# A third buffer for the decay factors of a selective scan, in SBUF beside two in PSUM

## The reference, cut to what matters

```python
A_bar = jnp.exp(delta[..., None] * A)                 # decay factors
Bx = delta[..., None] * Bm[:, :, None, :] * xb[..., None]
def step(h, inp):
    a_t, bx_t, c_t = inp
    h = a_t * h + bx_t
    y_t = jnp.sum(h * c_t[:, None, :], axis=-1)
    return (h, y_t)
...
y = y + xb * Dp
out = y * jax.nn.silu(z) @ W_out
```

## Time and profile before

| | |
|---|---|
| time, median of 3 runs | 2658.17 us (2652.7 to 2659.58) |
| the profiled execution | 2653.91 us, its span 2651.9 us |
| VectorE busy | 2265.5 us (85%) |
| TensorE busy | 2309.5 us (87%) |
| GpSimd busy | 1728.4 us (65%) |
| ScalarE busy | 1669.0 us (63%) |
| granted TensorE clock, mean | 0.95 of full speed |

### The profile page before, as it was taken

How to read it: one execution, slowest core, us unless ns; L and a number is a source line. 1 busy time by engine, 2 the same in 40 slices (tenths; PEclk the granted TensorE clock), 3 DMA queues, 4 the chain that set the end, 5 groups by cost and what they waited for, 6 DMA issues and landing times. The chain is left out here.

```text
span 2651.9 us, 34212 instructions
## 1 busy us (share of the span) xinstructions
PE 2309.5 (87%) x11520; PEld 1586.2 (60%) x11520; DVE 2265.5 (85%) x2232; ACT 1669.0 (63%) x3332; POOL 1728.4 (65%) x2042
## 2 busy tenths in 40 slices
PE   7778889888898988888988888888888875999997
PEld 5566667676666666757666666666666322444443
DVE  2399999999999999899999999999999835888886
ACT  2567676667667676767676767676766534555554
POOL 0278787878787878778787778787878711222221
PEclk8889999999999999999999999999998987999999
DMA  4102020202010110102020202020104621111110
GB/s 186 72 1 72 9 76 6 76 5 80 16 65 21 61 53 28 65 17 73 9 72 10 72 10 72 10 76 5 72 10 189 233 83 56 60 64 66 59 52 24
DMA packets 48299, 151.74 MB, mean 57 GB/s; under 512 B 8069, under 2 KB 8965, under 8 KB 45198
## 3 DMA queue, kind: packets, MB, share of 16 engines
q1 hardware_dynamic: 48142, 149.76, 15.9%
HBM read 132.37 MB, written 17.37 MB: 56 GB/s over the span
## 5 line engine op out<-in xcount | busy, mean ns | idle before, releaser
L472 POOL TENSOR_TENSOR ring<-ring,Cbc 128x512 f32<-128x512 f32 x1024 | 1283.1, 1275 | 44.5 <-POOL carry L465 0.4
L864 DVE TENSOR_TENSOR_SCAN ring<-a_ps,ring 128x1024 f32<-128x1024 f32 x512 | 1168.0, 2281 | 106.7 <-ACT a_ps L702 105.2
L702 ACT ACTIVATE a_ps<-delta,nA 128x255 f32<-128x255 f32 x2048 | 852.9, 468 | 380.3 <-DVE ring L864 379.4
L1069 PE MATMUL yT_ps<-ident,ring 128*128 128x128 f32 x4096 | 588.1, 284 | 163.5 <-POOL ring L472 160.0
L1069 PEld LDWEIGHTS yT_ps<-ident,ring 128*128 128x128 f32 x4096 | 475.0, 145 | 282.2 <-POOL ring L472 241.9
L856 DVE TENSOR_TENSOR ring<-u_ps,Bbc 128x1024 f32<-128x1024 f32 x512 | 619.7, 1210 | 16.0 <-PE yT_ps L1069 9.3
L1035 PE MATMUL work<-xb,big 128*128 128x256 f32 x2048 | 476.8, 385 | 10.1 <-ACT zs L560 10.1
L1035 PEld LDWEIGHTS work<-xb,big 128*128 128x128 f32 x2048 | 385.5, 193 | 79.5 <-issue 16.9
L465 POOL TENSOR_TENSOR carry<-ring,half 128x4 f32<-128x4 f32 x512 | 127.1, 248 | 361.2 <-DVE ring L864 359.7
L1051 PE MATMUL work<-Wout,xb 128*128 128x512 f32 x512 | 237.7, 599 | 0.0
L1414 POOL TENSOR_TENSOR m<-m,pows 128x1 f32<-128x1 f32 x64 | 34.2, 549 | 311.4 <-DVE m L1546 311.4
(11 more groups left out here) (197 smaller groups left out, 2508.1 us busy)
## 6 DMA issues: line engine op xcount, KB each, us to landing
Bbc<-bc_rows SPq DMA_DIRECT2D x64, 512.0 KB, 4.6
Cbc<-bc_rows SPq DMA_DIRECT2D x64, 512.0 KB, 3.7
xT<-in_xT SPq DMA_DIRECT2D x16, 514.0 KB, 3.5
x_rows<-x2row SPq DMA_DIRECT2D x32, 256.0 KB, 2.0
xp<-x_rows SPq DMA_DIRECT2D x32, 256.0 KB, 2.7
xx<-in_x SPq DMA_DIRECT2D x32, 256.0 KB, 3.0
out_rows<-orow SPq DMA_DIRECT2D x32, 256.0 KB, 2.0
delta<-in_c_w SPq DMA_DIRECT2D x6, 1024.0 KB, 5.3
```

What stands on the lines that cost most here:

```text
L472: nc.gpsimd.tensor_tensor(hp, hp, Cbc[:, G * g + GP * c:G * g + GP * c + GP, :], ALU.mult)\
L702: r = nc.scalar.activation(a_ps[q % 2][:, i, 1:T], delta[:, par, dt, 1:T], ACT.Exp, scale=nA[:, dt, s:s + 1])
L864: dve.tensor_tensor_scan(ring[:, q % RING, :, :].rearrange("p g t -> p (g t)"), a_ps[q % 2][:, :, :].rearrange("p g t -> p (g t)"), ring[: ...
L1069: r = pe.matmul(yT_ps[:, tt, :], ring[:, q % RING, i, P * tt:P * tt + P], ident[:, :], is_transpose=True, start=False, stop=(g == NG - 1 a ...
```

## The change

A third decay buffer `a_sb` is laid into columns 6144 to 7167 of `big[0]`, in SBUF. The slots take the three buffers in turn by the running slot number, so every third slot uses the one in SBUF. ScalarE's wait goes from the scan of slot q - 2 to that of q - 3. `y0k`, which lay in these columns, moves to columns 5632 to 6143. The f_w1 piece for columns 6144 to 7167 is now sent after the last scan. The first column of the new buffer is cleared once.

```diff
-        y0k = big[0][:, 6 * DI:6 * DI + 2 * T].rearrange("p (b t) -> p b t", b=2)
+        y0k = big[0][:, 5 * DI + D:6 * DI].rearrange("p (b t) -> p b t", b=2)
+        a_sb = big[0][:, 6 * DI:7 * DI].rearrange("p (g t) -> p g t", g=G)
...
+        a_of = [a_ps[0], a_ps[1], a_sb]
+        NA = len(a_of)
...
-                        if 2 <= c < 9:
+                        if 2 <= c < 8:
...
+                    sp.wait_ge(s_scan, NQ * NBLK)
+                    sp.dma_start(big[0][:, 6 * DI:7 * DI], f_w1[:, 6 * DI:7 * DI]).then_inc(s_big[0], 16)
...
-                        act.wait_ge(s_aclr, 3)
-                    wait(act, s_scan, NQ * k + q - 1)
+                        act.wait_ge(s_aclr, 4)
+                    wait(act, s_scan, NQ * k + q - NA + 1)
...
-                        r = nc.scalar.activation(a_ps[q % 2][:, i, 1:T], delta[:, par, dt, 1:T], ACT.Exp,
+                        r = nc.scalar.activation(a_of[(NQ * k + q) % NA][:, i, 1:T], delta[:, par, dt, 1:T], ACT.Exp,
...
-                                           a_ps[q % 2][:, :, :].rearrange("p g t -> p (g t)"),
+                                           a_of[(NQ * k + q) % NA][:, :, :].rearrange("p g t -> p (g t)"),
...
+                        dve.memset(a_sb[:, :, 0:1], 0.0).then_inc(s_aclr, 1)
```

## The result

The changed kernel takes 2809.7 us in the median (2808.7 to 2812.06, 4 runs) against 2656.8 of the kernel before, run beside it (2652.7 to 2659.58, 4 runs): 1.0578 times as long, 95% interval 1.056 to 1.0596, or 153 us more. The forecast was 2785, with 2655 to 2880 as its range. The forecast rise of 127 us came out as 153.

The account below looks back on a forecast made before the run. VectorE was followed as the bounding engine, with GpSimd becoming full too. VectorE's 94 us and GpSimd's 67 us gave a middle of 127, other parts 0: 2653.9 + 127 = 2781 profiled, 2785 median, range 2655 to 2880.

Parts of the forecast that it names:

- The run-ahead gives nothing: ScalarE's longer run-ahead: 0 to 10 of VectorE's 93.7 us waits for factors come back, taken as 0.
- The scan is held as L835 is: Scans with two SBUF operands and GpSimd's multiplies block each other, like u product L835; GpSimd loses 2.05 us a scan.
- VectorE's own wait: VectorE's 170 scans with two SBUF operands each wait 0.55 us for GpSimd's running multiply: 94 us.
- GpSimd's term: GpSimd loses 349 us against 340.0 of reserve, 58 of it unusable: 9 + 58 = 67 us rise by GpSimd alone.
- The sum: Whole kernel: 127 us, the middle between 94 (stalls fall together) and 161 (they add), on 2653.9 profiled.
- ScalarE's writes into SBUF: ScalarE's activations for every third slot take 468 ns into SBUF as into PSUM: 0.
- y0k, the memset, the moved f_w1 piece: Moved copy, one start-up memset and a weight piece sent after the last scan, landing before it is wanted: 0.
- the scan that isn't held: Rival at VectorE's SBUF scans: they stay at 2.28 us, total 2648 to 2658, or 2564 at best; chance 0.14.
- Held but covered: Rival: scans are held but the waits fall into idle time, +9 us or less, 2658 to 2667; chance 0.05.
- GpSimd keeps its turn: Rival: a scan waits to the end of GpSimd's multiply pair, 1.73 us each, 294 us, 2952; chance 0.07.
- The fourth: Rival: GpSimd's delay reaches TensorE, then ScalarE, stretching each block's 3.6 us stall; 32 us on top, 2817; no chance given.

Follow-up runs that it names:

- e2_psum_constant: Changed kernel, but every third slot's scan reads a constant column in PSUM instead of the third buffer; run-ahead kept: 2653.2 us, 0.9981 of the kernel before.
- e1_no_runahead: Changed kernel with ScalarE's wait put back to the scan of slot q - 2; every third slot still reads factors from SBUF: 2820.8 us.
- e4_silu_later: Kernel before, with ScalarE's SiLU moved from slot 17 to slot 18, behind the factors of slot 17: 2654.3 us, 0.9987.
- e8_every_fifth: Changed kernel with only every fifth slot's factors in SBUF (102 scans), without the longer run-ahead: 2738.8 us, 1.0299 of the kernel before.
- e3_every_second: Changed kernel with every second slot's factors in SBUF (256 scans), without the longer run-ahead: 2871.0 us, 1.0793 of the kernel before.
- e11_after_xdp: Changed kernel with the product of xb and Dp moved from GpSimd to ScalarE: 2786.3 us, 1.0491 of the kernel before.
- e7_short_after: Changed kernel with GpSimd multiplying only 128 of 256 positions: 2671.3 us; the kernel before with the same short multiply: 2608.2 us.
- e5_swapped: Against the kernel before: both factor buffers in SBUF, products of u and B in PSUM, ring of three slots: 2673.8 us, 1.0051.
- e12_after_memset: Changed kernel with GpSimd's multiply replaced by a memset that writes SBUF and reads nothing: 2576 us, one run.

## Why the prediction was right

- **The run-ahead gives nothing, since the late factors hang on TensorE.** Right. With the collision away it gives 5 us, inside the 0 to 10 (e2_psum_constant), with the collision 6 to 11 (e1_no_runahead), and the waits for factors are 93.7, 93.6 and 92.4 us with two buffers, three, and three with the collision. The step from the earlier trace rows, to ask what ended ScalarE's own idle time in front of the late factors, is what told this in advance. e4_silu_later adds that ScalarE's order can move these waits, but not the time.
- **The scan is held as L835 is.** Right, in form and in the size of one stop: 1.98 us for a pair, forecast 2.05; VectorE's scans from 2.28 to 3.55 us, forecast 2.28 to 3.4.
- **VectorE's own wait, 0.55 x 170 = 94 us.** Too large: 0.39 x 170 = 66 us. I had counted every scan as meeting a multiply. 22 of the 170 took 2.31 us or less, and the other 148 stood 0.45 us in the mean. The fastest on `big` take the old 2.28 us; one such comes at 1233.44, one product behind a 1.59 us wait of VectorE in which GpSimd had caught up. With the u product and the small L755, which I had let cancel or not seen, it is 82 us.
- **GpSimd's term, half of 67 us.** The step that was mis-sized, and its reasoning was wrong too. I let GpSimd lose time until its 340 us of reserve were gone, then took half of what was over, 33 us. Measured are 68 us of new waits for `yT_ps`, and GpSimd still has 235.6 us of waiting for scans, with 256 us lost and not 349 (1.5 us a scan and not 2.05). The doses show that this part doesn't start at a threshold: it is 35 us at 102 scans already (e8_every_fifth), and no larger than 39 at 256 (e3_every_second). e11_after_xdp shows that GpSimd's lateness has a share in it, and e7_short_after that it does not go away when GpSimd has 700 us to spare. What counts, as I read it, is when a state is late for the gate two slots on, and the block has a gate every four slots.
- **The sum.** The rise came within 26 us of the forecast partly by luck. VectorE's stops were put 12 us too high and the waits 35 us too low, and half of 67 us had no ground but being the middle of two cases.
- **ScalarE's writes into SBUF, 0.** The two rows that I compared differ in where they read. The same instruction of the changed kernel takes 469 ns into `a_ps` and 501 ns into `big`:

```profile
L707 ACT ACTIVATE a_ps<-delta,nA 128x255 f32<-128x255 f32 x1340 | 554.1, 469 | 38.6 <-DVE ring L869 38.1
L707 ACT ACTIVATE big<-delta,nA 128x255 f32<-128x255 f32 x668 | 283.5, 501 | 34.4 <-DVE ring L869 34.2
```

  The page of the Trainium skill that I weighed ("ScalarE: Activation LUTs", section "Step-by-step: what each stage is for") was right and my reading of the rows wrong, by 32 ns. It stayed without effect on the time, as e2_psum_constant, which has these writes too, shows.
- **y0k, the memset, the moved f_w1 piece: 0.** Right for the time. The copy of y0k went from 0.356 to 0.423 us, 1 us in all.
- **The rivals.** The chances had a slip: of the 0.14 for the scan that isn't held, most was to be without a visible gain, yet 0.08 went to faster. Not held: out. Held but covered: out, by a wide margin. GpSimd keeps its turn: out. VectorE gets in between the halves, as at 1206.51. The fourth, that GpSimd's delay goes on through TensorE, is what the second part of the cost is, at 68 us of new waits where I gave it 32; but it came back at the gates and the ring, not as a longer wait for factors.

One thing stays open. TensorE's mean granted clock is 0.928 of full speed after and 0.950 before, and its delta product (L1035, now L1041) takes 398 ns in the mean against 385. Over the program TensorE is busy for 55 us more with the same matmuls (2364.7 us against 2309.5), and it also waits longer for GpSimd, 272 us against 153. Whether the lower clock adds to the lateness of the states wasn't separated; e8_every_fifth, with a clock of 0.948, costs 0.78 us a scan and e1_no_runahead, with 0.924, costs 0.95, which would fit, but e3_every_second has 0.931 and 0.83.

## What to carry to other kernels

Four things carry over, as far as one kernel can show them. Before adding a buffer, look at what ends the idle time of the engine that fills it, in the stretch just before the late piece: if that is a third engine, the buffer only moves the waiting. Before moving an operand, look at where the other operand of its reader lies. The VectorE instructions that read two tensors from SBUF took turns here with GpSimd's instructions that read SBUF, and the stop is hidden in busy time, so look for instructions of one shape whose longest time is far above their median. Idle time of an engine isn't a reserve that can be spent anywhere: a hand-over that comes late cost time here even though GpSimd was idle for 29% of it. And an experiment that swaps operands changes waits as well, so read its price from the groups and the timeline and not from the time alone.

## What the runs showed of the hardware

- A VectorE instruction with one SBUF tensor as input can be held too: L755, 64x256 in place in SBUF with a scalar, took 0.259 us before and 0.716 in the mean after, 1.291 in e3_every_second. The copy of y0k, SBUF to SBUF, rose as well, from 0.356 to 0.423; in e5_swapped it took 0.267. The Trainium skill ("SBUF — State Buffer", section "Who interferes with whom") names this kind, `tensor_scalar` and copies in the modes that use both ports, and the rows agree.
- The product of u and B takes 1.20 us in the profile where it starts about 0.08 us before the end of the scan in front of it, and 1.23 us where it starts after that end. The kernel before has both kinds, all writing SBUF, with a mean of 1.210; in e5_swapped, where it writes PSUM and waits for the scan, the mean is 1.232. So that difference does not show a price of writing PSUM.
- What holds a scan with two SBUF operands need not be a multiply: the 2.34 us product on `delta` made one last 4.35 us (e12_after_memset).
- The same scan takes 2.278 us whichever of its two operands is in PSUM.
